# The second aggregation's sums on TensorE: one-hots held, gathered rows moving, and each sum turned afterwards

## The reference

```python
def _graph_conv(x, W, b, edge_src, edge_dst, edge_weight, num_nodes):
    support = x @ W
    msgs = support[edge_src] * edge_weight[:, None]
    return segment_sum(msgs, edge_dst, num_nodes) + b

h = relu(_graph_conv(layernorm(x), W1, b1, ...))      # 128 features
x = x + _graph_conv(h, W2, b2, ...)                   # the second aggregation
n = layernorm(x)
top_w, top_i = top_k(softmax(relu(n @ r1 + rb1) @ r2 + rb2), 2)
h1 = relu(n @ w1[e] + b1[e]); h2 = relu(h1 @ w2[e] + b2[e])   # six experts e
x = x + sum over the top 2 of softmax(top_w) * (h2 @ w3[e] + b3[e])
```

## Time and profile before

| | |
|---|---|
| median of 3 runs | 4281.37 us (4277.43 to 4283.28) |
| profiled execution, first to last instruction (its span) | 4272.1 us |
| profiled execution, its own time | not given apart; the median is 9.3 us above the span |
| busy over the whole span | PE 3514.0 us (82%), DVE 2295.0 (54%), ACT 1939.7 (45%), POOL 2823.4 (66%) |
| mean granted TensorE clock | 0.848 |
| `stage_mixing` | about 1291 to 2527 us |

### The profile page before, as it was taken

One profiled execution on the slowest core, in us unless ns is written; L12 is line 12 of the kernel. 1 busy time (PEld: TensorE's weight loads), 2 busy tenths in 40 slices (PEclk: granted clock), 3 DMA queues, 4 the chain that ended last, 5 costly groups with the idle time before them and its releaser, 6 DMA issues. The chain is left out here.

```text
span 4272.1 us, 68475 instructions
## 1 busy us (share of the span) xinstructions
PE 3514.0 (82%) x17723; PEld 3093.3 (72%) x17723; DVE 2295.0 (54%) x6976; ACT 1939.7 (45%) x3024; POOL 2823.4 (66%) x2732
## 2 busy tenths in 40 slices
PE   4777777777756899999999968888888888649999
PEld 4666666666645788888888867777777777538887
DVE  6566556556554445545445436666666666632222
ACT  4455555555541333333333445555555555423333
POOL 3677777777767777766676227777777777353444
PEclk7788788888776999999999987777777787559999
DMA  6455555555543222222222126666666666534443
GB/s 177 154 187 188 179 174 183 178 180 178 178 140 107 69 68 66 69 66 64 68 67 64 36 96 208 212 206 212 209 209 208 212 211 191 172 137 92 98 98 60
DMA packets 287817, 605.53 MB, mean 142 GB/s; under 512 B 61999, under 2 KB 163342, under 8 KB 287499
## 3 DMA queue, kind: packets, MB, share of 16 engines
q1 hardware_dynamic: 166267, 344.34, 25.0%
q0 software_dynamic: 114784, 245.67, 21.0%
q10 hardware_dynamic: 6576, 13.36, 0.9%
HBM read 460.33 MB, written 144.67 MB: 142 GB/s over the span
## 5 line engine op out<-in xcount | busy, mean ns | idle before, releaser
L1669 POOL DMA_INDIRECT y_node<-node_table,src_sb x832 | 847.6, 1019 | 379.2 <-issue 378.9
L509 POOL DMA_INDIRECT conv_gath<-support_table,src_sb x832 | 878.4, 1056 | 284.3 <-issue 259.9
L1110 POOL DMA_INDIRECT x_gath<-hidden_table,src_sb x832 | 792.9, 953 | 353.6 <-issue 259.9
L664 PE MATMUL conv_pz<-conv_we,conv_edge 128*128 128x256 f32 x2240 | 643.1, 451 | 76.9 <-PEq L97 76.7
L1682 PE MATMUL y_pa<-y_hot,y_node 128*128 128x64 f32 x3328 | 523.6, 326 | 181.7 <-PEq L97 181.1
L1682 PEld LDWEIGHTS y_pa<-y_hot,y_node 128*128 128x128 f32 x3328 | 506.8, 240 | 214.7 <-issue 212.0
L664 PEld LDWEIGHTS conv_pz<-conv_we,conv_edge 128*128 128x128 f32 x2240 | 510.2, 234 | 170.2 <-issue 81.4
L655 PE MATMUL conv_ps<-conv_hot,conv_gath 128*128 128x64 f32 x1664 | 255.6, 305 | 213.5 <-DMA conv_gath<-support_table,src_sb 210.9
L655 PEld LDWEIGHTS conv_ps<-conv_hot,conv_gath 128*128 128x128 f32 x1664 | 242.5, 219 | 245.9 <-DMA conv_gath<-support_table,src_sb 238.5
L1734 ACT ACTIVATE y_node<-y_node 128x1024 f32<-128x1024 f32 x208 | 219.4, 1056 | 340.6 <-ACTq L97 340.1
L1692 PE MATMUL y_pz<-y_we,y_edge 128*128 128x256 f32 x1104 | 361.0, 499 | 13.0 <-PEq L97 13.0
(11 more groups left out here) (256 smaller groups left out, 5844.8 us busy)
## 6 DMA issues: line engine op xcount, KB each, us to landing
conv_edge<-in_edge_t SPq DMA_DIRECT2D x140, 512.0 KB
edge_mish_table<-conv_neg SPq DMA_DIRECT2D x140, 512.0 KB
y_neg<-edge_mish_table SPq DMA_DIRECT2D x139, 512.0 KB, 4.2
y_edge<-in_edge_t SPq DMA_DIRECT2D x69, 512.0 KB
e_rows<-expert_rows SPq DMA_DIRECT2D x56, 272.0 KB, 3.3
conv_gath<-support_table,src_sb POOLq DMA_INDIRECT x832
x_gath<-hidden_table,src_sb POOLq DMA_INDIRECT x832
y_node<-node_table,src_sb POOLq DMA_INDIRECT x832, 3.1
```

Of the source, the lines that this page charges most:

```text
L509: pool.indirect_dma_start(gath[g % SLOTS][:, j, :], None, table[:, :], bass.IndirectOffsetOnAxis(ap=c.src[:, col:col + 1], axis=0),).then_ ...
L664: last = pe.matmul(ps_z[r % 2][:, j, :], edge[r][:, m, j * P:(j + 1) * P], we[:, m, :], start=m == 0, stop=m == KD - 1)
L1110: pool.indirect_dma_start(gath[g % SLOTS][:, j, :], None, table[:, :], bass.IndirectOffsetOnAxis(ap=c.src[:, col:col + 1], axis=0),).then_ ...
L1669: pool.indirect_dma_start(node[g % SLOTS][:, j, :], None, c.t3[:, :], bass.IndirectOffsetOnAxis(ap=c.src[:, col:col + 1], axis=0),).then_i ...
```

## The change

The two operands of `segment` change places: the one-hots, now 66 columns wide (`WP`; the two new columns are zero), are held and the gathered rows [128 edges, 128 features] move, so that the sum comes out as [66 nodes, 128 features] in a single PSUM tile `ps`. ScalarE copies it to the single SBUF tile `held` (`copied_sum`), which also frees `ps` and the gather slot; TensorE transposes it into the single PSUM tile `pw` [128, 66] (`turned_sum`); VectorE adds 64 columns of that. TensorE turns the first sum of a step after the next expert's first layer, then forms the second sum if there is one, and turns that after the second layer. ScalarE copies the first sum at the head of the step and the second after the first layer's ReLU. VectorE adds the first at the head and the second ahead of `weighted`, behind that step's other work. In the groups before the first step each sum is turned at once; ScalarE's wait for `first_in` comes after them.

```diff
--- before.py
+++ after.py
@@ -38,6 +38,7 @@
 BEFORE = ((0, 1), (2,), (3, 4), (5,))
...
 TW = NP + W
+WP = W + 2
 EPS = 1e-5
...
 E1 = 8
@@ -999,7 +1000,8 @@
         rel = sb("rel", [P, C])
...
         gath = [sb(f"gath{s}", [P, CG, HID]) for s in range(SLOTS)]
-        hot = [sb(f"hot{half}", [P, HALF_COLS, W]) for half in range(2)]
+        hot = [sb(f"hot{half}", [P, HALF_COLS, WP]) for half in range(2)]
+        held = sb("held", [WP, HID])
         at_hot = [sb(f"at_hot{half}", [P, 2, HALF_COLS]) for half in range(2)]
...
         b_l, iota8, w_d, b_d = sb("b_l", [P, E0]), sb("iota8", [P, 8]), sb("w_d", [P, KD, D]), sb("b_d", [P, D])
@@ -1019,13 +1021,14 @@
         at, is_nth, top = sb("at", [P, 2, PIECE]), sb("is_nth", [P, 2, PIECE, 8]), sb("top", [P, PIECE])
...
         shares = sb("shares", [P, PIECE, P])
-        ps = [pb(f"ps{n}", [P, W]) for n in range(2)]
+        ps, pw = pb("ps", [WP, HID]), pb("pw", [P, WP])
         pt, ph, pm = (pb(n, [P, KD, PIECE * P]) for n in ("pt", "ph", "pm"))
...
         gathered = [nc.alloc_semaphore(f"x_gathered{s}") for s in range(SLOTS)]
-        hot_ready, ps_ready, ps_free = ([sem(f"{n}{r}") for r in range(2)] for n in ("hot_ready", "ps_ready", "ps_free"))
+        hot_ready, ps_ready, ps_free = [sem(f"hot_ready{r}") for r in range(2)], sem("ps_ready"), sem("ps_free")
+        held_ready, pw_ready, pw_free = sem("held_ready"), sem("pw_ready"), sem("pw_free")
         slot_free, added = sem("slot_free"), sem("added")
...
         first_in, w_in, consts_ready = sem("first_in"), sem("w_in"), sem("consts_ready")
@@ -1053,7 +1056,9 @@
             if not 0 <= u + 1 < U - 1:
...
             begin, end = DUE[u + 1], DUE[u + 2]
-            return range(begin + (end - begin) * j // E0, begin + (end - begin) * (j + 1) // E0)
+            now = range(begin + (end - begin) * j // E0, begin + (end - begin) * (j + 1) // E0)
+            assert len(now) <= 2
+            return now
...
             return (u, e + 1) if e + 1 < E0 else (u + 1, 0)
@@ -1116,16 +1121,21 @@
         @block.tensor
...
             def segment(k, g):
-                s, n, half, at = g % SLOTS, g % 2, g // 3 % 2, g % 3 * CG
+                s, half, at = g % SLOTS, g // 3 % 2, g % 3 * CG
                 if at == 0:
...
-                take(pe, ps_free[n])
+                take(pe, ps_free)
                 pe.wait_ge(gathered[s], k * ((IT - (s >= TAIL)) * CG * 16) + (g // SLOTS + 1) * CG * 16)
                 for j in range(CG):
-                    last = pe.matmul(ps[n][:], gath[s][:, j, :], hot[half][:, at + j, :], start=j == 0, stop=j == CG - 1)
-                last.then_inc(ps_ready[n], 1)
+                    last = pe.matmul(ps[:], hot[half][:, at + j, :], gath[s][:, j, :], start=j == 0, stop=j == CG - 1)
+                last.then_inc(ps_ready, 1)
+
+            def turned_sum():
+                take(pe, held_ready)
+                take(pe, pw_free)
+                pe.transpose(pw[:], held[:], c.ident[0:WP, 0:WP]).then_inc(pw_ready, 1)
...
                 take(pe, added)
@@ -1207,13 +1217,18 @@
                 last.then_inc(py_ready, 1)
             def step(k, u, j):
-                for g in summed_in(u, j):
-                    segment(k, g)
+                summed = summed_in(u, j)
+                if len(summed) > 0:
+                    segment(k, summed[0])
                 following, earlier = next_of(u, j), earlier_of(u, j)
...
                     first_layer(*following)
+                if len(summed) > 0:
+                    turned_sum()
+                if len(summed) > 1:
+                    segment(k, summed[1])
                 if j == 0 and there(u + 1):
...
                 if j == 1 and there(u - 2):
@@ -1327,7 +1345,17 @@
                     last = act.activation(mid[e % 2][:, m, 0:width(u)], pm[:, m, 0:width(u)], ACT.Relu, bias=b_2[:, e, m:m + 1])
...
+            def copied_sum():
+                take(act, ps_ready)
+                act.sem_inc(slot_free, 1)
+                link(act, act.copy(held[:], ps[:]), act_own)
+                act.sem_inc(ps_free, 1)
+                act.sem_inc(held_ready, 1)
+
             def step(u, j):
+                summed = summed_in(u, j)
+                if len(summed) > 0:
+                    copied_sum()
                 if j == 0 and there(u):
...
                 if j == 1 and (there(u + 1) or there(u - 1)):
@@ -1360,8 +1390,10 @@
...
             log_exp_table(act)
-            act.wait_ge(first_in, 16 * len(first))
             with act.Fori(0, load_passes(act)) as k:
+                for g in range(DUE[0]):
+                    copied_sum()
+                act.wait_ge(first_in, 16 * len(first))
                 for u in range(-1, U + 2):
...
                         step(u, j)
@@ -1375,19 +1407,18 @@
                 nc.vector.tensor_copy(at_hot[h % 2][:, 0, :], part_of(rel))
...
                 for j in range(HALF_COLS):
-                    last = nc.vector.scalar_tensor_tensor(hot[h % 2][:, j, :], c.iota[:], at_hot[h % 2][:, 0, j:j + 1],
+                    last = nc.vector.scalar_tensor_tensor(hot[h % 2][:, j, 0:W], c.iota[:], at_hot[h % 2][:, 0, j:j + 1],
                                                           at_hot[h % 2][:, 1, j:j + 1].to_broadcast([P, W]), ALU.is_equal, ALU.mult)
...
                     places[:] = places_of(nc, window, g, min(SLOTS, GROUPS - g), whole=True)
-                take(dve, ps_ready[g % 2])
-                dve.sem_inc(slot_free, 1)
+                take(dve, pw_ready)
                 here = c.sums[:, bass.ds(places[g % SLOTS], W)]
-                link(dve, nc.vector.tensor_tensor(here, here, ps[g % 2][:], ALU.add), own)
-                dve.sem_inc(ps_free[g % 2], 1)
+                link(dve, nc.vector.tensor_tensor(here, here, pw[:, 0:W], ALU.add), own)
+                dve.sem_inc(pw_free, 1)
                 if DUE.count(g + 1):
...
                 if g % 3 == 2 and g // 3 + 2 <= (GROUPS - 1) // 3:
@@ -1496,8 +1527,9 @@
                 dve.sem_inc(py_free, 1)
             def step(u, j):
-                for g in summed_in(u, j):
-                    add(g)
+                summed = summed_in(u, j)
+                if len(summed) > 0:
+                    add(summed[0])
                 if j == 0 and there(u - 2):
...
                 if j == 0 and there(u + 1):
@@ -1514,6 +1546,8 @@
                     bounded(u - 1)
...
                     chose(u + 1)
+                if len(summed) > 1:
+                    add(summed[1])
                 earlier = earlier_of(u, j)
...
                     weighted(*earlier)
@@ -1522,14 +1556,17 @@
                 if j == 0 and (there(u + 1) or there(u - 1)):
...
+            dve.sem_inc(ps_free, 1)
+            dve.sem_inc(pw_free, 1)
             for n in range(2):
-                dve.sem_inc(ps_free[n], 1)
                 dve.sem_inc(rows_out[n], 16)
...
             nc.vector.memset(ln2[:], LN2)
+            for half in range(2):
+                nc.vector.memset(hot[half][:, :, W:WP], 0.0)
             nc.vector.memset(shares[:], 0.0)
...
```

## The result

After the change the kernel takes **4303.73 us** (median of 4 runs, 4288.11 to 4305.46), before it 4279.4 us (4 runs, 4276.96 to 4283.28): a ratio of 1.0049 with an interval of 1.0033 to 1.0065, slower by half a per cent. The forecast was 4303 us.

A forecast was written before the change was run, and what follows sets the result against it. TensorE sets the pace from 1442 us, gathers before. 13.1 (turns outside the chain) + 3.9 + 6.6 - 1.3 = 22.3 us slower: 4294 in span, 4303 us by the median; own range 4292 to 4318, chance 0.52.

The forecast's parts named there:

- Half the load buys nothing: TensorE's x_ps: holding 66 columns instead of 128 leaves the slot at 0.111 us, since 128 columns now move; change 0.
- 17.2 us for 177 turns: TensorE after 1442 us: one added transpose a group, 129 at 0.112 and 48 at 0.058 us; bounds 10 and 50.
- rival 3: Turns stand exposed, from ScalarE or single ps, held and pw buffers: 44 us more, 4347 us; chance 0.17.
- ScalarE's copy is hidden: 177 copies of 66 x 128, about 0.27 us each, hidden behind the expert's first layer of 1.78 us.
- `support` after step 5: After step 5 of units 7, 12 and 19, late `added` makes TensorE wait 2.2 us, three times: plus 6.6 us.
- The chain to x_pt, plus 3.9 us: Changes by unit, 3 to 22, in the path from step 1's start to x_pt, including 4.1 us of turns: plus 3.9.
- Where the load holds `pw`: Units 7 and 19: step 1's second group has the register load, its late add holds `pw`: plus 1.3 and 0.4 us.
- Idle ahead of x_pt near 25 us again: Sign in the new profile: TensorE's idle before x_pt stays near 25 us, in other units, gone in 9 and 21.
- rival 2: All 25.6 us of idle ahead of x_pt goes as second adds leave the chain: minus 10, 4271 us; chance 0.09.
- First stretch, -1.3 us: Stretch paced by gathers: the later second sum swallows the last wait of 1.48 us; with some turns, minus 1.3 us.
- M + S + 4.74: Time from step 1's start to x_pt: M the moments, S the adds before the shares, plus 4.74 us.
- rivals, 1: Register load and `pw` never hold TensorE: plus 10 us or less, 4290, or 4286 with a shorter chain; chance 0.22.

The follow-up runs named there:

- turns_only: Kernel before plus one transpose of a constant 66-wide tile per group, read by nobody: 4287.36 us, ratio 1.0024; stage 1243.7 us against 1234.5.
- swap_only: Kernel before with only the sum's two operands exchanged, no turn or ScalarE copy: 4281.83 us (1 run); stage 1234.1 us against 1234.5.
- act_order: Kernel after, with ScalarE's second copy of step 1 moved ahead of `guessed`: 4293.79 us, ratio to before 1.0035; stage 1255.6 us.
- after_again: Kernel after, run and profiled once more unchanged: 4302.34 us, ratio to before 1.0063; stage 1257.7 us against 1261.1 in the first profile.
- places_early: Kernel after, with VectorE's six places read into registers behind `weighted` of steps 2 and 4: 4268.18 us, ratio to before 0.9978.
- order_only: Kernel before with only the new order: a step's second group formed behind the first layer and added ahead of `weighted`: 4264.09 us, ratio 0.9958.
- places_and_act: Kernel after with the early register read and ScalarE's second copy of step 1 ahead of `guessed`: 4261.03 us, ratio to before 0.9962.

## Why the prediction held, and which of its terms did not

- **TensorE is the bound: shown.** `turns_only` lengthens the stage with work that nobody waits for.
- **Half the load buys nothing: right.** Forecast 0.111 us a slot, measured 0.109 against 0.112 inside a run. The 3.6 us over 20 units were not in the sum, and `swap_only` shows that by themselves they don't shorten the stage.
- **17.2 us for 177 turns: right.** 16.3 us for 168 of them in `turns_only`, where 16.3 would be 168 / 177 of the forecast. The slot of 0.11 is the one that was read from x_pt, and the 0.06 an estimate that a turn ahead of x_ps bears out (0.062 to the next start); the full record of 0.28 (rival 3's price) was never paid in the stream.
- **ScalarE's copy is hidden: right in size, wrong in one place.** 260 ns, as estimated. But in step 1 the second copy waits behind `guessed` in ScalarE's queue. Unit 11 was forecast with it, at plus 1.2 us, and gave 2.2; `act_order` shows it in units 3 and 15 too, 4 us in all.
- **`support` after step 5: right.** Waits of 2.27, 1.51 and 1.31 us from the starts, 5.1 together, for 6.6, at the three units named.
- **The chain to x_pt, plus 3.9 us: right but for the clock, which is the term that the sum lacks.** Measured from step 1's start to x_pt over the same 20 units: plus 10.9, and plus 7.6 in `after_again`. Of that 6.4 and 3.5 are half clock, where the kernel before has none on this stretch; the rest is 4.5 and 4.1. Before, the half clock came behind x_pt, since the long waits were there. Now the long waits stand at turns in step 1, and what is slow behind them lies on the way to x_pt. Sixteen of the units came out within 0.7 us. Unit 5 gave plus 3.0 for 0.3, of which 2.9 are half clock; in `after_again`, with the same wait at its turn and a full clock, it gave 0.35. Units 15 and 17 gave plus 1.8 and 2.7 for -0.6 and 0.3, with 1.7 of half clock each. Unit 11 gave 2.2 for 1.2 with none: that is ScalarE's place.
- **Where the load holds `pw`: missed in two units, and nearly free there.** The forecast counted `pw` as held by a late add in units 7 and 19 and missed that the same holds in 5 and 17, where the load is with the *first* add of step 1 and a second turn follows. VectorE is late with x_pt in these units anyway, so TensorE waits at the turn instead: unit 5 lost 3.9 us to waits on this stretch before and 3.6 after. `places_early` shows the cause of the wait by removing it: there the turn of unit 5 waits 1.14 us, with ScalarE's place mended too nothing. That the load costs much in both kernels was in the forecast's rows, but not that moving it would pay.
- **Idle ahead of x_pt near 25 us again: wrong.** It fell to 9.0. The order alone takes 11 us of it (`order_only`), and what TensorE now waits at a turn it no longer waits at x_pt. Relief of 16 us is just the point that rival 2 named for its turn to faster. It was reached, and the new waits at the turns, 22.7 us, took it back.
- **First stretch, -1.3 us: about right.** From the first x_ps to x_pt of unit 2 it is 152.9 us before, 152.2 after.
- **A constant that doesn't come out of its rows.** The chain is given as M + S + 4.74, but in unit 14, from which it is told, 11.13 - 2.80 - 3.25 leaves 5.08. In units 12, 20 and 22 the trace has 4.73 from the first shares instruction to x_pt. The difference is 0.3 us, and little hangs on it, since changes were summed.
- **4272.1 + 22 = 4294 in span, 4303 by the median: the right number for a wrong reason.** Runs list 1.8 us between span and time (4286.3 and 4288.11), not 9: the profiled execution before took some 4274 us, less than each of the three timed ones. Added to the median, 22.3 gives 4303.7, and the medians rose by 24.3. The luck lies in how close they meet: the stage grew by 26.6 us in one profile and by 23.2 in the other, and the half clock makes nearly all of that difference.

Set beside the forecast, which has no clock in it: over the 20 units it had 13.1 + 3.9 + 6.6 = 23.6 us, and measured without the half clock are 22.9 (28.6 - 5.7) and 22.3 (24.8 - 2.5).

Of the rivals, 1 is out: the load holds `pw`, and does so oftener than forecast. 2 is out for the change as made but describes `places_and_act`, for another reason than it gave. 3 is out: 12 turns of 175 wait, and none pays its record.

Open: what decides whether the clock falls behind a long wait, and so whether an execution of this kernel pays 2.5 or 5.7 us for it, as its two profiles did. A second buffer `pw` wasn't tried.

## What to carry to other kernels

Price small products that are added to a stream from start to start, over the whole run and the first record behind it: a record of 0.22 us cost 0.10. Then ask of each single buffer who frees it and what stands in that engine's queue ahead of the release; here an unrelated read of six registers, 3 to 4 us of VectorE's queue, held the buffer, and moving it was worth more than the whole change. Look at the granted clock behind each long wait, not at its mean over a stage: here a quarter to a third of what moving the load gained was half clock, which the view of waits doesn't list. When a change bundles an operation with a reordering, time the reordering alone on the old kernel: here it was the only part that gained.

## What the runs showed that was not expected

- Reading six places into VectorE's registers keeps the following add 3.2 to 4.0 us behind the last instruction (1699.31 to 1702.49, 1562.77 to 1566.75), though the load itself is listed at a median of 1.4 us.
- Between 1442 and 2430 us TensorE's clock fell to half 2 to 6 times in eight of the eleven traces, each time during or right behind a wait of 2.0 to 3.5 us, and never in the three in which the longest wait there is 1.4 us. Two traces of one kernel differ in it by 3.2 us.
- With 66 columns held and 128 moving, eight x_ps records take 0.873 us; with 128 held and 64 moving 0.838, but then the x_ph records behind them take 0.054 more. The two sides of a product cost nearly the same here.
- A stage that no edit touches, the first convolution, varied by 16 us between the profiled executions (1130 to 1146 us), more than half of what the change costs.
